# Thirty of 1661 gathers of edge rows, fetched row by row from SyncE's queue instead of by GpSimd

## The chip, the cores and the metric

The kernel runs on one core of a Trainium2 chip. The metric is the device time of one execution in microseconds (us); the runs of one kernel are summed up by their median.

## What is computed

A graph layer, a linear-attention mixer and a mixture of experts over 12500 nodes of 256 features. The change lies in the graph layer, with 212500 edges that are sorted by destination:

```python
h = einsum('ni,hif->hnf', x, W)                    # 8 heads of 32
s_src, s_dst = einsum('hnf,hf->hn', h, a_src), einsum('hnf,hf->hn', h, a_dst)
ea = leaky_relu(s_src[:, src] + s_dst[:, dst]).T   # one score per edge and head
ea = exp(ea - segment_max(ea, dst)[dst])
ea = ea / (segment_sum(ea, dst)[dst] + EPS)
out = segment_sum(hn[src] * ea[:, :, None], dst)   # sum over a node's edges
```

The mixer's result and the layer's input are added, and the sum goes through eight experts, two per node.

## The kernel before, in words

The program has three stages with a barrier between them. In the first, each node gets a row of 272 numbers in a table in memory (`table`: 256 features, 16 scores). In the second, the edge stage, the edges are taken in 104 groups of 16 chunks of 128 edges. In the third, nodes are routed to experts, and the experts run.

The edge stage is written out by hand, engine by engine:

- GpSimd (`edges_pool`, L1232) gathers the 128 table rows of each chunk with one indirect DMA, by row numbers that lie in `srcix`. There are three buffers `rows`, one per group (`NR` = 3); the gather of chunk j of group k waits until PE has summed chunk j of group k - 3.
- ScalarE (`copy_scores`, L1348) copies the scores out of a group's rows once all 16 gathers have landed; for group k + 2 it does so at the end of its iteration k. PE transposes them (L1296), VectorE makes edge scores and maxima and weighs the rows (L1463), PE sums each chunk with a one-hot matrix (L1314), ScalarE copies the sums out (L1370) and sends them to memory (L1395, L1398).
- SyncE (`edges_sync`) has one iteration per group. It loads the edge numbers of group k + 2 (`dsr`, L1260), takes three steps of other work, reads a flag (`anyfar`, L1273) that tells whether a node in this group has so many edges that its sums have to be moved, and takes a fourth step.

The other work is that of the mixer: on every engine, `Beside` takes steps of the mixer's weights (L821), its network with 25 blocks of nodes (on SyncE L1015 loads, L1020 stores, L1032 loads) and of the merge behind it. The steps are counted, so that a step stands at the same place of the groups on all engines. SyncE waits in its one stream: what stands behind a wait is issued after it.

```python
for k in range(GROUPS):
    if NR <= k + 2 < GROUPS:
        edge_ids(sp, S, B, k + 2)
    for _ in range(3):
        beside()
```

Of the kernel before, what the change touches and what calls it, by code (L numbers as in the profile page):

```python
# [63 lines left out]

LAG, TURN_LAG, TURN_GAP = 7, 12, 7

ROUNDS = [list(range(k, min(k + 2, NS))) for k in range(0, NS, 2)]
# [69 lines left out]
class Sems:  # L139
    def __init__(self, nc):  # L140
        new = nc.alloc_semaphore
        several = lambda name, n: [new(f"{name}{i}") for i in range(n)]
        self.stage = new("stage_done")
        self.const = new("constants")
        self.vec = new("vector_chain")

        self.ix_in, self.ix_rows, self.ix_fl = new("ix_in"), new("ix_ends_out_in"), new("ix_first_last")
        self.ix_tp, self.ix_cp, self.ix_num = new("ix_turned"), new("ix_copied"), new("ix_numbers")
        self.ix_hot, self.ix_hist, self.ix_sums = new("ix_hot_ready"), new("ix_histogram"), new("ix_sums")

        self.a_w, self.a_x, self.a_xt, self.a_h = new("a_weights_in"), several("a_x_in", NXB), several("a_xt_in", NXB), several("a_h_out", NXB)
        self.wcat, self.a_zero = new("wcat_ready"), new("frag_zeroed")
        self.xn, self.xnt, self.xt, self.h, self.hr, self.gram = (new(n) for n in (
            "norms_ready", "rows_turned", "xt_copied", "h_done", "h_copied", "gram_done"))
        self.gcopy = new("gram_copied")

        self.mix_in, self.mixp, self.mixv, self.mixa = new("mix_in"), new("mix_tensor"), new("mix_vector"), new("mix_scalar")

        self.es_in, self.es_sd, self.es_tp = new("ends_in"), new("ends_scores_copied"), new("ends_moved")

        self.rows_in, self.ds_in = several("rows_in", NR), several("ds_in", NR)
        self.near, self.far = several("near_out", 2), several("far_out", 2)
        (self.sce, self.tsc, self.flags, self.oh, self.inb, self.eav, self.fm, self.exp, self.tw, self.tail, self.wgh,
         self.sum, self.ev) = (new(n) for n in (
            "scores_copied", "scores_turned", "flags_ready", "onehot_ready", "scores_free", "edge_scores", "maxima_ready", "weights_exp",
            "weights_turned", "tails_ready", "rows_weighed", "chunk_summed", "chunk_copied"))

        self.m_w, self.m_xs, self.m_xt, self.m_o = new("m_weights_in"), new("m_x_in"), new("m_xt_in"), new("m_out")
        (self.m_pre, self.m_ready, self.m_q, self.m_x2, self.m_hn, self.m_tp, self.m_t, self.m_f1, self.m_g, self.m_f2, self.m_y,
         self.m_x3) = (new(n) for n in (  # L170
            "m_bias_sum", "m_weights_ready", "m_q_done", "m_x2_ready", "m_hn_ready", "m_hn_turned", "m_hnt_copied", "m_fc1_done",
            "m_gelu_done", "m_fc2_done", "m_y_added", "m_x3_ready"))

        self.mg_in, self.mg_out = new("mg_in"), new("mg_out")
# [12 lines left out]
        self.e_endrow, self.planned = new("e_end_rows"), new("planned")  # L187

        self.x_w1, self.x_w, self.x_b = new("x_first_weights_in"), new("x_second_weights_in"), new("x_biases_in")
        self.x_in, self.x_y, self.x_wt = several("x_in", NI), several("x_out", NOUT), new("x_first_weights_copied")  # L190
        self.x_wc, self.x_bc = several("x_wc_in", NW), several("x_bc_in", NB)
        (self.x_tp, self.x_gt, self.x_f1, self.x_h, self.x_f2, self.x_st, self.x_aim) = (new(n) for n in (
            "x_turned", "x_in_copied", "x_fc1_done", "x_gelu_done", "x_fc2_done", "x_y_read_scaled", "x_aimed"))
# [80 lines left out]
class Bufs:  # L274


    def __init__(self, nc, a, out):
# [17 lines left out]
        self.wqa, self.bqa = A("wqa", [P, KD, D], F32), A("bqa", [P, D], F32)  # L295
        self.dfb, self.dlb, self.loc = A("dfb", [GH, CHUNKS], F32), A("dlb", [GH, CHUNKS], F32), A("loc", [P, CHUNKS], F32)
        self.srcix, self.sdedge = A("srcix", [P, CHUNKS], I32), A("sdedge", [P, 2, GROUPS], F32)
        self.begins = A("ends_begins", [P, BLOCKS], F32)
        self.norm = A("norm", [P, 2, TILES], F32)
        self.far, self.anyfar, self.islast = A("far", [1, CHUNKS], I32), A("anyfar", [1, GROUPS], I32), A("islast", [P, CHUNKS], BF16)  # L300
        mark = nc.sbuf_base
        self.fli = A("dfl_i", [P, 2, BLOCKS], I32)
        mark_ix = nc.sbuf_base

        self.rows = several("rows", NR, [P, CB, ROW])
# [3 lines left out]
        self.onehot = several("onehot", 2, [P, CB, P])  # L309
        mark_ends = nc.sbuf_base  # L310
        self.ends, self.sd = A("ix_rows", [P, BLOCKS, ROW], F32), A("ix_sd", [P, 2, BLOCKS, GH], F32)
        ends_end, nc.sbuf_base = nc.sbuf_base, mark_ends
        self.fout = several("fout", 2, [P, CB, ROW])
        mark_edges = nc.sbuf_base
# [17 lines left out]
        self.wcat, self.avec = A("wcat", [P, KD, ROW], F32), A("avec", [P, 2, D], F32)  # L332
        self.xs, self.st_a = several("xs", NXB, [P, 2 * ST, D]), A("st_a", [P, 2 * ST, 16], F32)
        self.xt, self.hr = several("xt", NXB, [P, KD, ST * P]), several("hr", NXB, [P, ST, ROW])
        self.shift = A("ix_shift", [P, 2 * P], F32)

        nc.sbuf_base = mark_edges
        self.dsr, self.sc_e = several("dsr", NR, [P, 2, P], I32), several("sc_e", 2, [P, 2, P])
# [15 lines left out]
        self.m_xt, self.m_x2 = A("m_xt", [P, KD, ST * P], F32), several("m_x2", 2, [P, ST, D])  # L354
        self.m_hn, self.m_xs = (A(n, [P, ST, D], F32) for n in ("m_hn", "m_xs"))
        self.m_hnt, self.m_hid, self.m_st = A("m_hnt", [P, KD, ST * P], F32), A("m_hid", [P, MT, ST * P], F32), A("m_st", [P, ST, 16], F32)

        nc.sbuf_base = mark_mlp
        self.first, self.last = several("mg_first", 2, [P, 4, ROW]), several("mg_last", 2, [P, 4, ROW])
# [865 lines left out]
def edges_pool(p, S, B, groups):  # L1225
    for k in groups:
        b = k % NR
        for j in range(min(CB, REAL - k * CB)):
            col = k * CB + j
            if k >= NR:  # L1230
                p.wait_ge(S.sum, (k - NR) * CB + j + 1)
            p.indirect_dma_start(out=B.rows[b][:, j, :], out_offset=None, in_=B.table[:, :],  # L1232
                                 in_offset=bass.IndirectOffsetOnAxis(ap=B.srcix[:, col:col + 1], axis=0)).then_inc(S.rows_in[b], 16)
# [26 lines left out]
        sp.dma_start(B.dsr[b][:, j, :], bass.AP(of.tensor, k * CB * P, [[P, CB], [0, GH], [1, P]])).then_inc(S.ds_in[b], 16)  # L1260


def edges_sync(sp, S, B):
    beside = Beside(mix_sync(sp, S, B), mlp_sync(sp, S, B), merge_sync(sp, S, B))
    for k in range(GROUPS):
        if NR <= k + 2 < GROUPS:
            edge_ids(sp, S, B, k + 2)
        for _ in range(3):
            beside()

        b = k % 2
# [69 lines left out]
def edges_scalar(a, S, B):  # L1341
    beside = Beside(mix_scalar(a, S, B), mlp_scalar(a, S, B), merge_scalar(a, S, B))

    def copy_scores(k):
        r, b = k % NR, k % 2
        a.wait_ge(S.rows_in[r], 16 * (CB * (k // NR) + min(CB, REAL - k * CB)))
        a.wait_ge(S.tsc, max(k - 1, 0))
        a.activation(B.sc_e[b][:, :, :].rearrange("p j (c h) -> p j c h", h=GH),  # L1348
                     B.rows[r][:, :, D:ROW].rearrange("p c (j h) -> p j c h", h=GH), ACT.Copy).then_inc(S.sce, 1)
# [1116 lines left out]
    late(route_scalar(a, S, B), experts_scalar(a, S, B))  # L2466


def sync_program(sp, S, B):
    nodes_sync(sp, S, B)  # L2470
    barrier(sp, S, 1)
    for k in range(NR):
        edge_ids(sp, S, B, k)
    edges_sync(sp, S, B)
    barrier(sp, S, 2)
    late(route_sync(sp, S, B), experts_sync(sp, S, B))
    for q in range(NF):
        sp.wait_ge(S.e_x1[q], max(stored_to(r) for r in range(q, len(ROUNDS), NF)))
    for u in range(NOUT):
        sp.wait_ge(S.x_y[u], added_to(max(range(u, SLOTS, NOUT))))  # L2480


def build(nc, a, out):
# [2 lines left out]
    vector_program(nc.vector, S, B)  # L2486
    tensor_program(nc.tensor, S, B)
    scalar_program(nc.scalar, S, B)
    sync_program(nc.sync, S, B)


_INS = ["x", "src", "dst", "L0_gnn_W", "L0_gnn_a_src", "L0_gnn_a_dst", "L0_mix_w_qkv", "L0_mix_b_qkv",
# [26 lines left out]
```

## Time and profile before

| | us |
|---|---|
| median of 3 runs | 3769.97 |
| lowest and highest run | 3769.4, 3783.53 |
| span of the profiled execution, first to last instruction | 3246.6 |
| median less span | 523.4 |

The profiled execution's own time is not listed beside its span. In the span, PE is busy 81%, GpSimd 69%, VectorE 62% and ScalarE 48%; the edge stage runs from about 153 us to 2290 us.

Rows of the trace name line, engine (PE and PEld for TensorE's products and weight loads, DVE for VectorE, ACT for ScalarE, POOL for GpSimd, SP for SyncE; a q behind it is the engine's sequencer, which issues DMAs and does register work), operation, output<-input and count.

### The profile page before, as it was taken

How to read it: one execution, taken by the hardware profiler on the slowest of the kernel's cores; microseconds unless marked ns; L12 is line 12 of the kernel's file. 1: busy time of each engine (PE TensorE's matmuls, PEld its weight loads, DVE VectorE, ACT ScalarE, POOL GpSimd, SP SyncE). 2: the span in 40 equal slices, each digit the busy share in tenths (PEclk: the TensorE clock that was granted, in tenths of full speed). 3: DMA queues.
4: the chain of work that ended last, by engine and by line, in shares of the span. 5: the costliest groups of instructions: out<-in, count | busy, mean ns of one | idle time of the engine just before them, and what ended most of it. 6: DMA issues, size and time to landing. Idle time of an engine off the chain costs nothing.

```text
span 3246.6 us, 42100 instructions
## 1 busy us (share of the span) xinstructions
PE 2642.4 (81%) x11512; PEld 2052.3 (63%) x11512; DVE 2010.3 (62%) x5442; ACT 1549.7 (48%) x3382; POOL 2234.9 (69%) x2193
## 2 busy tenths in 40 slices
PE   8657767888888888888888887566359999999998
PEld 6546655666666665666656656344247888778887
DVE  7446557667777676777767766677654555445422
ACT  5325544544555554555455554334234545545444
POOL 0277777777777777777777777776476767676554
PEclk9879988999999999999999998777569999999999
DMA  9797766566666666666566665565766676766663
GB/s 276 242 295 211 199 178 169 162 173 177 164 172 180 172 172 170 174 179 171 163 180 172 173 169 153 160 181 136 253 198 146 151 160 148 162 142 131 131 110 62
DMA packets 397637, 561.15 MB, mean 173 GB/s; under 512 B 71912, under 2 KB 317950, under 8 KB 397225
## 3 DMA queue, kind: packets, MB, share of 16 engines
q0 software_dynamic: 123696, 298.61, 36.3%
q1 hardware_dynamic: 196473, 170.69, 18.1%
q10 hardware_dynamic: 77159, 88.50, 10.4%
q8 instruction: 99, 1.62, 0.2%
q14 instruction: 210, 1.72, 0.2%
HBM read 402.42 MB, written 169.68 MB: 176 GB/s over the span
## 4 chain that ended last, share of the span: by engine, by line
PE 65%; DMA 10%; ACT 8%; POOL 8%; issue 6%; DVE 2%; ACTq 0%; SPq 0%; POOLq 0%; DVEq 0%
PE bank L1314 21%; PE bank L2295 11%; PE bank L2308 10%; DMA rows<-table,srcix 9%; PE bank L1095 7%; POOL rows L1232 6%; PE bank L1084 5%; PE bank L1057 2%; PE bank L865 1%; PE bank L605 1%; PE bank L606 1%; ACT L1354 1%; PE bank L2284 1%; ACT xg L842 1%; PE bank L1296 1%
## 5 line engine op out<-in xcount | busy, mean ns | idle before, releaser
L1232 POOL DMA_INDIRECT rows<-table,srcix x1661 | 1600.3, 963 | 506.4 <-issue 354.2
L1314 PE MATMUL bank<-rows,onehot 128*128 128x272 f32 x3328 | 928.6, 426 | 57.4 <-ACT fout L1370 52.0
L1370 ACT ACTIVATE fout<-bank 128x272 f32<-128x272 f32 x1659 | 638.6, 397 | 574.7 <-PE bank L1314 525.3
L1314 PEld LDWEIGHTS bank<-rows,onehot 128*128 128x128 f32 x3328 | 666.5, 208 | 244.3 <-ACT fout L1370 78.7
L1463 DVE TENSOR_TENSOR rows<-rows,bank 128x1024 f32<-128x1024 f32 x416 | 484.0, 1213 | 173.2 <-ACT rows L1359 172.8
L2386 POOL DMA_INDIRECT out<-x_y,x_dest x203 | 325.0, 1601 | 233.2 <-DMA out<-x_y,x_dest 173.4
L2295 PE MATMUL bank<-x_int,x_w1c 128*128 128x256 f32 (+1 forms) x1696 | 379.7, 378 | 25.5 <-issue 22.2
L2308 PE MATMUL bank<-e_w,x_ht 128*128 x1624 | 370.5, 381 | 9.5 <-issue 7.0
L2295 PEld LDWEIGHTS bank<-x_int,x_w1c 128*128 128x128 f32 x1696 | 316.4, 194 | 77.4 <-issue 35.6
L2334 ACT ACTIVATE x_ht<-bank,x_b1c 128x256 f32<-128x256 f32 (+1 forms) x424 | 173.1, 462 | 394.4 <-PE bank L2295 392.9
L2308 PEld LDWEIGHTS bank<-e_w,x_ht 128*128 128x128 f32 x1624 | 300.2, 190 | 51.3 <-issue 14.8
L1084 PE MATMUL bank<-m_hnt,fc_w 128*128 128x512 f32 (+1 forms) x600 | 284.0, 598 | 17.1 <-ACT m_hid L1200 17.1
L2363 DVE TENSOR_TENSOR x_y<-bank,x_b2c 128x512 f32<-128x512 f32 (+1 forms) x106 | 70.8, 668 | 341.1 <-PE bank L2308 341.1
L1296 PE MATMUL bank<-ident,sc_e 128*128 128x128 f32 x104 | 38.4, 369 | 286.4 <-ACT sc_e L1348 275.4
L1095 PE MATMUL bank<-fc_w,m_hid 128*128 128x256 f32 x1176 | 270.8, 382 | 0.0
L1436 DVE SCALAR_TENSOR_TENSOR g_sdm<-notself,bank 128x128 f32<-128x128 f32 x104 | 30.0, 288 | 360.6 <-PE bank L1297 360.1
L1348 ACT ACTIVATE sc_e<-rows 128x256 f32<-128x256 f32 x104 | 43.3, 416 | 435.4 <-DMA rows<-table,srcix 417.3
L1095 PEld LDWEIGHTS bank<-fc_w,m_hid 128*128 128x128 f32 x1176 | 226.1, 192 | 34.2
L1771 POOL DMA_INDIRECT sorted_d<-e_hn,e_row x196 | 195.5, 997 | 64.9 <-issue 58.2
L1428 DVE TENSOR_TENSOR onehot<-bank,loc 128x2032 f32<-128x2032 f32 x104 | 235.6, 2266 | 0.2
L1296 PEld LDWEIGHTS bank<-ident,sc_e 128*128 128x128 f32 x104 | 16.4, 158 | 326.2 <-ACT sc_e L1348 313.7
L1084 PEld LDWEIGHTS bank<-m_hnt,fc_w 128*128 128x128 f32 x600 | 118.0, 198 | 112.3 <-issue 74.4
(405 smaller groups left out, 3246.3 us busy)
## 6 DMA issues: line engine op xcount, KB each, us to landing
frag<-fout ACTq DMA_DIRECT2D x104, 544.0 KB
rows<-table,srcix POOLq DMA_INDIRECT x1661
x_in<-sorted_d SPq DMA_DIRECT2D x97, 260.0 KB, 3.5
x_b2c<-in_L_ffn_b SPq DMA_DIRECT2D x106, 128.0 KB, 3.5
frag<-in_x ACTq DMA_DIRECT2D x1, 13416.0 KB
table<-hr SPq DMA_DIRECT2D x24, 544.0 KB, 4.0
xs<-in_x SPq DMA_DIRECT2D x24, 512.0 KB, 6.0
xg<-in_x SPq DMA_DIRECT2D x24, 512.0 KB, 6.4
```

Source lines behind the costliest of these rows:

```text
L1084: t = pe.matmul(bank[own[m % 2]][:, 0:n * P], B.mw1[:, kk, m * P:(m + 1) * P], B.m_hnt[:, kk, 0:n * P], start=(kk == 0), stop=(kk == KD - 1))
L1095: t = pe.matmul(bank[own[i // 2]][:, i % 2 * D:(i % 2 + 1) * D], B.m_hid[:, m, i * P:(i + 1) * P], B.mw2[:, m, :], start=(m == 0), stop=(m ...
L1232: p.indirect_dma_start(out=B.rows[b][:, j, :], out_offset=None, in_=B.table[:, :], in_offset=bass.IndirectOffsetOnAxis(ap=B.srcix[:, col:c ...
L1314: pe.matmul(B.banks[2 + c % 3][:, 0:ROW], B.onehot[k % 2][:, j, :], B.rows[k % NR][:, j, :], start=True, stop=True).then_inc(S.sum, 1)
L1370: a.activation(B.fout[k % 2][:, j, :], B.banks[2 + c % 3][:, 0:ROW], ACT.Copy).then_inc(S.ev, 1)
L1428: v.tensor_tensor(B.onehot[b][:, :, 0:P - 1], B.banks[0][:, 2 * P:3 * P - 1].unsqueeze(1).to_broadcast([P, CB, P - 1]), B.loc[:, k * CB:(k ...
L1463: v.tensor_tensor(h, h, w.unsqueeze(3).to_broadcast([P, n, GH, GF]), ALU.mult).then_inc(S.wgh, 1)
L1771: p.indirect_dma_start(out=B.sorted_d[:, :], out_offset=bass.IndirectOffsetOnAxis(ap=B.e_row[:, j, at:at + 1], axis=0), in_=B.e_hn[r % NH] ...
L2295: t = pe.matmul(out, B.w1c[u][:, k, m * P:(m + 1) * P], B.gt[u][:, k, 0:n], start=(k == 0), stop=(k == KD - 1))
L2308: t = pe.matmul(bk[BANKS_OUT[u]][:, i * D:(i + 1) * D], B.ht[u][:, m, i * P:(i + 1) * P], B.w2[:, bass.ds(ex * HT + m, 1), :], start=(m == ...
L2334: a.activation(B.ht[u][:, m, 0:n], B.banks[BANKS_H[m * 2 // HT]][:, m % 2 * ET:m % 2 * ET + n], ACT.Gelu, bias=B.b1c[w][:, m:m + 1]).then_ ...
L2386: p.indirect_dma_start(out=B.out[:, :], out_offset=bass.IndirectOffsetOnAxis(ap=B.dest[j % (NOUT + 1)][:, i:i + 1], axis=0), in_=B.y[j % N ...
```

## The change

SyncE fetches the first chunk of 30 groups: group 4 and every third after it, up to group 91. GpSimd leaves these chunks out.

Before the first group, three loads put the row numbers of the 30 chunks in partitions 1 to 3 of `far`. In three iterations of SyncE, nine steps are taken for one chunk, one ahead of each of the three beside steps: eight that load 16 row numbers into 16 registers and issue 16 DMAs of one row each into a buffer `hand` (two of these), and a ninth that waits for the 128 rows and for the group's buffer, and copies them to their place. The chunk of group k = 4 + 3i is fetched in the iterations 3i to 3i + 2, that is k - 4 to k - 2. The values carry no range check. ScalarE's copy of the scores of such a group also waits for the move. Three small tensors are put elsewhere in the on-chip memory to make room.

```diff
+HAND_FIRST, HAND_EVERY, HANDS = 4, 3, 30
+HAND_PART = 16
...
 def edges_pool(p, S, B, groups):
     for k in groups:
         b = k % NR
-        for j in range(min(CB, REAL - k * CB)):
+        for j in range(0 if hand_of(k) is None else 1, min(CB, REAL - k * CB)):
...
+def hand_sync(nc, sp, S, B):
+
+    step = HAND_EVERY * CB * P
+    for row in range(HAND_ROWS):
+        first, n = row * HAND_IDS, min(HAND_IDS, HANDS - row * HAND_IDS)
+        sp.dma_start(B.far[1 + row:2 + row, 0:n * P].rearrange("o (c e) -> o c e", e=P),
+                     bass.AP(B.src.tensor, HAND_FIRST * CB * P + first * step, [[step * n, 1], [step, n], [1, P]])).then_inc(S.ix_in, 16)
+    sp.wait_ge(S.ix_in, 32 + 16 * HAND_ROWS)
+    for i in range(HANDS):
+        b, row, at, k = i % 2, 1 + i // HAND_IDS, i % HAND_IDS * P, HAND_FIRST + i * HAND_EVERY
+        if i >= 2:
+            sp.wait_ge(S.sce, k - 2 * HAND_EVERY + 1)
+        for part in range(HAND_PARTS):
+            e0 = part * HAND_PART
+            _, ids = nc.values_load_multi_w_load_instructions(
+                B.far[row:row + 1, at + e0:at + e0 + HAND_PART], engines=[mybir.EngineType.SP], min_val=0, max_val=N_PAD - 1,
+                skip_runtime_bounds_check_because="ids of the padded table's rows")
+            for e, of in enumerate(ids, e0):
+                sp.dma_start(B.hand[b][e:e + 1, :], B.table[bass.ds(of, 1), :]).then_inc(S.hand_rows[b], 16)
+            yield
+        sp.wait_ge(S.hand_rows[b], 16 * P * (i // 2 + 1))
+        sp.wait_ge(S.sum, (k - NR) * CB + 1)
+        sp.dma_start(B.rows[k % NR][:, 0, :], B.hand[b][:, :]).then_inc(S.hand, 16)
+        yield
...
         for _ in range(3):
+            next(hand, None)
             beside()
...
-        a.wait_ge(S.rows_in[r], 16 * (CB * (k // NR) + min(CB, REAL - k * CB)))
+        a.wait_ge(S.rows_in[r], gathered_to(k))
+        if hand_of(k) is not None:
+            a.wait_ge(S.hand, hand_moved(hand_of(k)))
```

SyncE's stream where the edge stage begins, before: the edge numbers of three groups, then the mixer's first loads.

```order
L1260 DMA dsr<-in_dst 128x1x128
L1260 DMA dsr<-in_src 128x1x128
L821 DMA xg<-in_x 128x4x256 x2
L826 DMA wqkv_s<-in_L_mix_w_qkv 128x2x768
L827 DMA bqkv_row<-in_L_mix_b_qkv 1x768
```

The same place of SyncE's stream in the change (`far` holds the row numbers; ISA is the register operation that makes an address, FUSED_REGOPS in the profile):

```order
L1282 DMA dsr<-in_dst 128x1x128
L1282 DMA dsr<-in_src 128x1x128
L1290 DMA far<-in_src 1x13x128 x2
L1290 DMA far<-in_src 1x4x128
L1299 TENSOR_LOAD far
L1303 ISA
L1303 DMA hand<-table 1x272
L1303 ISA
L1303 DMA hand<-table 1x272
```

The pair of ISA and DMA stands there 16 times, then come the mixer's loads, then the next load of 16 numbers. In all the stream has 3840 such pairs, 240 loads and 30 moves more.

The end of a chunk in SyncE's stream of the change, in the third iteration:

```order
L1303 ISA
L1303 DMA hand<-table 1x272
L1307 DMA rows<-hand 128x272
L843 DMA xg<-in_x 128x4x256
L1323 TENSOR_LOAD anyfar
L1323 ISA x2
L1324 COMPARE_AND_BRANCH
```

The move is the last step of the chunk, ahead of the beside step and the flag of that iteration.

ScalarE's stream at the end of its iteration 2, before (with the semaphores that a row waits for):

```order
L1370 ACTIVATE fout0<-bank4 128x272 [waits chunk_summed]
L1395 DMA frag<-fout0 32x16x272 [waits chunk_copied]
L1398 DMA last_d<-fout0 1x4352
L1348 ACTIVATE sc_e0<-rows1 128x256 [waits scores_turned,rows_in1]
L1370 ACTIVATE fout1<-bank2 128x272 [waits chunk_summed,far_out1,near_out1]
```

And in the change:

```order
L1422 ACTIVATE fout0<-bank4 128x272 [waits chunk_summed]
L1447 DMA frag<-fout0 32x16x272 [waits chunk_copied]
L1450 DMA last_d<-fout0 1x4352
L1400 ACTIVATE sc_e0<-rows1 128x256 [waits scores_turned,a_xt_in_and_hand_moved0,rows_in1]
L1422 ACTIVATE fout1<-bank2 128x272 [waits chunk_summed,far_out1,near_out1]
```

The copy of the scores of group 4 waits for the move as well; behind it in ScalarE's stream stand the copies of the sums of group 3. On GpSimd, the row of 1661 gathers has become one of 1631.

## Rows read from the trace of the kernel before

**Rows 1.** Busy time by stretch: length, then each engine's busy us (instructions), PE's granted clock, DMA share, GB/s.
```profile
core 0: us, PE busy (x) PEld busy (x) DVE busy (x) ACT busy (x) POOL busy (x), PEclk, DMA share, GB/s
153.00:2243.00 2090.00, 1660.96 (x6611) 1225.70 (x6612) 1422.00 (x3113) 1021.05 (x2341) 1587.36 (x1649) 0.90 0.64 178
...
1080.00:2010.00 930.00, 794.62 (x3131) 582.28 (x3130) 658.66 (x1490) 486.13 (x1066) 706.01 (x735) 0.94 0.62 171
2010.00:2290.00 280.00, 173.38 (x654) 126.58 (x652) 197.85 (x382) 107.24 (x282) 191.03 (x193) 0.78 0.57 153
```

**Rows 2.** The gathers, by tile (ns min/median/max, first and last start) and in the page's groups.
```profile
L1232 POOL DMA_INDIRECT rows<-table,srcix x1661: 942/949/1988, 153.3 to 2258.6; - x185
...
L1232 POOL DMA_INDIRECT rows<-table,srcix x1661 | 1600.3, 963 | 506.4 <-issue 354.2
```

**Rows 3.** Who waited for whom: us in total, times, longest us.
```profile
ACT sc_e L1348 <- DMA rows<-table,srcix: 417.3, 82, 50.0
...
PE bank L1296 <- ACT sc_e L1348: 275.4, 65, 17.4
...
POOL rows L1232 <- PE bank L1314: 152.1, 499, 0.3
```

**Rows 4.** The same view for SP's own queue.
```profile
SPq L1015 <- PE bank L1057: 648.4, 24, 32.5
SPq L1020 <- DVE m_x L1153: 554.2, 25, 45.2
...
SPq L821 <- PE bank L865: 208.7, 22, 46.9
```

**Rows 5.** Lines L1830 and L1831 on SP: ns min/median/max, first and last start us.
```profile
L1830 SPq TENSOR_LOAD <-pl_endrow x8: 267/270/1007, 3073.5 to 3082.1; - x8
L1830 SPq FUSED_REGOPS  x8: 152/152/156, 3073.8 to 3082.4; - x8
...
L1831 SPq FUSED_REGOPS  x8: 37/37/42, 3074.0 to 3082.7; - x8
L1831 SPq DMA_DIRECT2D sorted_d<-pl_zero x8: 332/332/383, 3074.2 to 3082.9; - x8
...
DMA to landing us min/median/max: 2.1/3.2/4.5
```

**Rows 6.** SP's DMA issues in order of time (start, us), 1008 to 1042; line L1273.
```profile
1010.26 0.60 SPq L1260 DMA_DIRECT2D dsr<-in_src  x1
1036.02 0.38 SPq L1020 DMA_DIRECT2D xm_d<-m_x  x1
1036.44 0.50 SPq L1032 DMA_DIRECT2D m_xs<-in_x  x1
1038.41 0.59 SPq L1260 DMA_DIRECT2D dsr<-in_dst  x1
...
1040.55 0.55 SPq L1260 DMA_DIRECT2D dsr<-in_dst  x1
1041.14 0.60 SPq L1260 DMA_DIRECT2D dsr<-in_src  x1
...
L1273 SPq TENSOR_LOAD <-anyfar x104: 262/278/1197, 218.2 to 2255.8; - x104
```

**Rows 7.** Issues of other lines: ns min/median/max, first and last start us.
```profile
L732 SPq DMA_DIRECT2D dfb<-rows_d x1: 270/270/270, 48.1 to 48.1; - x1
L732 SPq DMA_DIRECT2D dlb<-rows_d x1: 298/298/298, 48.4 to 48.4; - x1
...
L1398 ACTq DMA_DIRECT2D last_d<-fout x103: 357/363/543, 224.1 to 2272.9; - x103
...
L1020 SPq DMA_DIRECT2D xm_d<-m_x x25: 370/378/383, 628.6 to 2027.9; - x25
L1032 SPq DMA_DIRECT2D m_xs<-in_x x25: 500/505/2418, 546.6 to 1972.7; - x25
...
L1521 SPq DMA_DIRECT2D mg_last<-fout x1: 603/603/603, 2284.0 to 2284.0; - x1
```

More of the change, by code:

```diff
@@ L65, with hand_of @@
 LAG, TURN_LAG, TURN_GAP = 7, 12, 7
+HAND_FIRST, HAND_EVERY, HANDS = 4, 3, 30
+HAND_PART = 16
+HAND_PARTS = P // HAND_PART
+HAND_IDS = CHUNKS // P
+HAND_ROWS = -(-HANDS // HAND_IDS)
+def hand_of(k):
+    i, off = divmod(k - HAND_FIRST, HAND_EVERY)
+    return i if off == 0 and 0 <= i < HANDS else None
 ROUNDS = [list(range(k, min(k + 2, NS))) for k in range(0, NS, 2)]
@@ L121, in added_to, with gathered_to, hand_moved @@
     return sum(16 * SUBS[i] for i in range(j % NOUT, j + 1, NOUT))
+def gathered_to(k):
+    return sum(16 * (min(CB, REAL - g * CB) - (hand_of(g) is not None)) for g in range(k % NR, k + 1, NR))
+def hand_moved(i):
+    return 16 * len(LOADED[0::NXB]) + 16 * (i + 1)
 def rows_of(a, s, n):
@@ L149, in __init__ @@
         self.ix_hot, self.ix_hist, self.ix_sums = new("ix_hot_ready"), new("ix_histogram"), new("ix_sums")
-        self.a_w, self.a_x, self.a_xt, self.a_h = new("a_weights_in"), several("a_x_in", NXB), several("a_xt_in", NXB), several("a_h_out", NXB)
+        self.a_w, self.a_x, self.a_xt, self.a_h = new("a_weights_in"), several("a_x_in", NXB), several("a_xt_in_and_hand_moved", NXB), several("a_h_out", NXB)
         self.wcat, self.a_zero = new("wcat_ready"), new("frag_zeroed")
@@ L161, in __init__ @@
         self.rows_in, self.ds_in = several("rows_in", NR), several("ds_in", NR)
+        self.hand_rows, self.hand = several("hand_rows_in", 2), self.a_xt[0]
         self.near, self.far = several("near_out", 2), several("far_out", 2)
@@ L297, in __init__ @@
         self.srcix, self.sdedge = A("srcix", [P, CHUNKS], I32), A("sdedge", [P, 2, GROUPS], F32)
-        self.begins = A("ends_begins", [P, BLOCKS], F32)
         self.norm = A("norm", [P, 2, TILES], F32)
-        self.far, self.anyfar, self.islast = A("far", [1, CHUNKS], I32), A("anyfar", [1, GROUPS], I32), A("islast", [P, CHUNKS], BF16)
-        mark = nc.sbuf_base
-        self.fli = A("dfl_i", [P, 2, BLOCKS], I32)
+        self.far, self.anyfar, self.islast = A("far", [1 + HAND_ROWS, CHUNKS], I32), A("anyfar", [1, GROUPS], I32), A("islast", [P, CHUNKS], BF16)
         mark_ix = nc.sbuf_base
@@ L311, in __init__ @@
         self.ends, self.sd = A("ix_rows", [P, BLOCKS, ROW], F32), A("ix_sd", [P, 2, BLOCKS, GH], F32)
+        self.begins, self.fli = A("ends_begins", [P, BLOCKS], F32), A("dfl_i", [P, 2, BLOCKS], I32)
+        self.shift = A("ix_shift", [P, 2 * P], F32)
         ends_end, nc.sbuf_base = nc.sbuf_base, mark_ends
@@ L334, in __init__ @@
         self.xt, self.hr = several("xt", NXB, [P, KD, ST * P]), several("hr", NXB, [P, ST, ROW])
-        self.shift = A("ix_shift", [P, 2 * P], F32)
         nc.sbuf_base = mark_edges
@@ L356, in __init__ @@
         self.m_hnt, self.m_hid, self.m_st = A("m_hnt", [P, KD, ST * P], F32), A("m_hid", [P, MT, ST * P], F32), A("m_st", [P, ST, 16], F32)
+        self.hand = several("hand", 2, [P, ROW])
         nc.sbuf_base = mark_mlp
@@ L1260, in edge_ids, with edges_sync @@
         sp.dma_start(B.dsr[b][:, j, :], bass.AP(of.tensor, k * CB * P, [[P, CB], [0, GH], [1, P]])).then_inc(S.ds_in[b], 16)
-def edges_sync(sp, S, B):
+def hand_sync(nc, sp, S, B):
[21 more added lines that the diff above has]
+        yield
+def edges_sync(nc, sp, S, B):
     beside = Beside(mix_sync(sp, S, B), mlp_sync(sp, S, B), merge_sync(sp, S, B))
+    hand = hand_sync(nc, sp, S, B)
     for k in range(GROUPS):
@@ L2466, in scalar_program, with sync_program @@
     late(route_scalar(a, S, B), experts_scalar(a, S, B))
-def sync_program(sp, S, B):
+def sync_program(nc, sp, S, B):
     nodes_sync(sp, S, B)
@@ L2473, in sync_program @@
         edge_ids(sp, S, B, k)
-    edges_sync(sp, S, B)
+    edges_sync(nc, sp, S, B)
     barrier(sp, S, 2)
@@ L2488, in build @@
     scalar_program(nc.scalar, S, B)
-    sync_program(nc.sync, S, B)
+    sync_program(nc, nc.sync, S, B)
 _INS = ["x", "src", "dst", "L0_gnn_W", "L0_gnn_a_src", "L0_gnn_a_dst", "L0_mix_w_qkv", "L0_mix_b_qkv",
```

## The prediction

> **What bounds the kernel now.** I read first the window table [rows 1]. The 2090 us from 153 to 2243 hold the edge stage, all but its last group; the node stage before and the expert stage behind keep their instructions, so the change is decided in this window. There POOL has 1587 us of busy time, PE 1661, DVE 1422, ACT 1021. None is full by that count, so the second view is the gathers themselves [rows 2]: 1661 of them start between 153.3 and 2258.6, one every (2258.6 - 153.3)/1660 = 1.268 us. The page's group gives the two parts of that pitch: 963 ns of work and 506.4 us of idle time over all gathers, 354.2 us of it "issue", the gap in which POOL waits for nothing. Third come the waits [rows 3]: ACT's copy of a group's scores waits 417 us for gathers that land, and PE's transposes of those scores wait for ACT; the other way, POOL waits 152 us for PE, in 499 pieces of at most 0.3 us. So POOL is the pacemaker: a group of 16 gathers lasts 20.29 us, three groups 60.9 us. A gather less is worth at most its pitch.
>
> SP has next to no work here, and yet is not free: it waits 648 us at L1015 (24 times), 554 us at L1020 and 209 us at L821 [rows 4], because the second network's loads and stores stand in its one stream at fixed steps beside the edges.
>
> **What the change removes.** 30 gathers of POOL: 30 x 1.268 = 38.0 us, if POOL stays the pacemaker and nothing arrives later. That is the whole possible gain, 1.0% of the time.
>
> **What it adds, all on SP's stream.** For one group in three, SP does the following in three of its iterations. In the meantime POOL uses 60.9 us, or 59.6 with the gather gone. What SP needs is the question.
>
> *128 row fetches.* Each is one FUSED_REGOPS (37 to 42 ns, [rows 5]), one DMA issue, and the gaps between instructions. A gap: the issue of dsr at 1040.55 lasts 0.55 and the next starts at 1041.14, so 0.04 us [rows 6]. The trace has no issue of one row with its address in a register. The nearest from above is L1831, 128 rows at a register's address, 332 ns [rows 5]; eight rows cost 270 and 298 (L732), the first one the lowest issue here [rows 7]. From below: L1398 is a piece of a single run, 363 ns, but stands right behind another issue. Such a place costs 0.505 - 0.378 = 0.127 us on SP (L1032 behind L1020), which leaves 0.236 us. I take 0.25, between 0.236 and 0.27, since a row has fewer parts than any of these. A row is then 0.04 + 0.25 + 2 x 0.04 = 0.37 us, 128 rows 47.4 us; the bounds are 45.6 us with 0.236 and 57.9 us with 0.332.
>
> *8 register loads of 16 numbers.* The trace has only loads of one number: 278 ns for L1273, 270 for L1830 [rows 5, 6]. If 16 come in one trip, the load costs 0.28 us; if they are 16 whole loads, 4.45 us. I expect one trip per number, because a one-number load takes seven times as long as the 37 ns register operation beside it, and only the trip to memory tells them apart. Of the 0.278 us I put down 0.152 (the other multi-step register instruction, [rows 5]) as what is paid once and 0.126 per number: 0.15 + 16 x 0.126 = 2.17 us. With its gap 2.21, times 8: 17.7 us. The bounds are 2.6 and 35.9 us.
>
> That is the least known term. The Trainium skill (Runtime: NRT & Kernel Launch, "Instruction fetch mechanics") says that a load into sequencer registers costs about 200 ns per register "even for bulk"; no run here shows a load of several. By it a load would be 3.2 us, the eight 25.9, and the kernel would end near 4416 us instead of the time below.
>
> *The wait and the move.* SP waits until the last row has landed: L1831's writes land 2.1 to 4.5 us after issue, 3.2 in the middle [rows 5]; the beside work in between hides a little, so 2.5 us. The move of 128 rows is one static issue, 0.5 us with its gap, priced like L1260. Its wait for the sum of an earlier group costs nothing as long as SP is the late one.
>
> *What SP does already.* Two dsr issues, the anyfar load and the branch: 2.14 us from 1038.41 to 1040.55, an iteration without anything else [rows 6], 6.4 us for three. The second network's three issues (0.378 + 0.378 + 0.505 and gaps) come 25 times in some 75 groups: 1.4 us for three groups.
>
> The sum: 47.4 + 17.7 + 2.5 + 0.5 + 6.4 + 1.4 = **75.9 us of SP against 60.9 us of POOL.** The move is waited for by ACT (the group's scores), ACT by PE, DVE and in the end POOL, whose buffers come free with PE's sums. So SP becomes the pacemaker, 15.0 us later with every hand, and the gathers saved on POOL are worth nothing: POOL then waits for buffers. Over 30 hands that is +450 us. Two credits: at the start SP sat up to 46.9 us at L821 [rows 4], so about 25 us of the first hand cost nothing; at the end POOL stands up to three buffers ahead, and the last twelve groups win back about 25 us before POOL paces again. Net +400 us: span 3246.6 + 400 = 3647 us.
>
> What else moves: the copy of 128 rows inside the chip and 30 gathers less are small beside the 0.64 DMA share [rows 1] and are covered by it; if rows on one queue were served late, the landing term grows. The three loads of row numbers lie ahead of the stage's first group and go with the start credit. The moved buffers cost nothing, no instruction hangs on their place. PE's share falls as SP paces; the window from 2010 to 2290, with PE busy 173 of 280 us, has a mean granted clock of 0.78, against 0.94 in the window before it with 795 of 930 [rows 1]. PE's 1661 us at 0.90 would be 1916 at 0.78, still under the 2490 us that the stage would then last, so I cost that at nothing; its cover is SP's own pace.
>
> The median of the runs shown is 3769.97 us, 523.4 us above the profiled span; the profiled execution's own time is not listed, so the median stands for it and these 523.4 us are held fixed. Forecast: 3769.97 + 400 = **4170 us**.
>
> **The rivals.**
> 1. *SP keeps up (faster).* If the 16 numbers come in one trip (2.6 us for eight) and a row costs 0.36 us or less, SP needs 45.6 + 2.6 + 10.8 = 59.0 us, under POOL's 59.6. It decides at 48.8 us for rows and loads together. Then the 38 us are had: 3732 us. For it: nothing in the trace forbids a cheap one-row issue or a block load. Against it: SP would be 99% full, and its stream still stops at L1015 and L1020 until PE and DVE have come to the same step (from about 1010.9 to 1036.0 in [rows 6]); every such stop would make a hand late. Chance 0.13.
> 2. *One trip per load, but SP just full.* Rows at 0.37, loads at 2.6: 60.8 us, to which the stops at L1015 and L1020 add some 2 us a hand on average, where one falls into the first iteration after a move, before PE has moved on. 62.8 - 60.9, times 30, less the 50 us of credits, is +7 us; with 5 us of stops +97. I put it at 3825 us, between the two; a row at 0.40 adds 3.8 us a hand and makes it 3940. Chance 0.24, of which 0.09 lies within 0.5% of the time before.
> 3. *Dearer than forecast.* 16 whole trips (35.9 us) give 94.1 us a hand, 30 x 33.2 - 50 = +946 us: 4716 us. Issues as dear as L1831's give 10.5 us more a hand: +315 us on any case. [...] Chance 0.13.
>
> That the change doesn't do what it says can be left out: the order of the instructions shows 1631 gathers, 3840 fetches and 30 moves.
>
> **How the numbers follow.** The forecast (SP paces, a trip per number, 1 to 3.3 us a load, its own range 3890 to 4600 us, the top with dearer rows) has chance 0.50. About 0.5%, some 19 us, is what a measurement can tell from no change here. Faster by more: rival 1, 0.13. Within: 0.09, from rival 2. Slower: 0.78. The range from 3725 to 4600 us takes in rivals 1 and 2 and the forecast's own range, and leaves out most of rival 3 and the tails.
>
> **What would show it.** Right: SP's fetches back to back, pitch near 0.37 us, with a load of about 2.2 us ahead of each 16; the waits at L1015 and L1020 nearly gone; ACT's score copies waiting long for the move's landing once in three groups, while POOL waits for PE's sums; a group pitch near 25 us up to group 91, then 20. Wrong: a load of 0.3 us or a row pitch under 0.36 (rivals 1, 2), POOL's pitch unchanged at 1.27 us with no new wait (rival 1), or the time outside the span growing with the longer program.

## The result, and the profile after the change

| | us |
|---|---|
| before, median of 4 runs (3763.11 to 3783.53) | 3769.68 |
| after, median of 4 runs (4749.42 to 4781.26) | 4764.19 |
| after / before | 1.2605, interval 1.2558 to 1.2652 |
| span of the profiled execution after, and its time | 4754.2, 4755.46 |

The change makes the kernel slower by 994.5 us, where +400 was forecast; the time lies above the range. The profiled execution ends 1.3 us after its span, so nothing like 523.4 us lies outside the span of a run; the profile of before that was shown, with its span of 3246.6 us, is that of an execution some 490 us or more shorter than every timed run.

SP's instructions for the hands in the changed kernel, by line (ns min/median/max, first and last start in us; L1299 loads 16 registers, L1303 fetches rows, L1307 moves them):

```profile
L1299 SPq TENSOR_LOAD <-far x240: 5/1159/3500, 165.1 to 3374.7; - x120
...
L1303 SPq FUSED_REGOPS  x3840: 1/37/1422, 166.3 to 3382.4; - x192
L1303 SPq MOVE hand<-table x3840: 1/29/1407, 166.4 to 3382.4; - x192
L1303 SPq DMA_DIRECT2D hand<-table x3840: 1/225/1696, 167.1 to 3382.5; - x192
...
L1307 SPq DMA_DIRECT2D rows<-hand x30: 533/542/1006, 320.0 to 3383.8; - x30
```

The 30 moves start from 320.0 to 3383.8: a hand takes (3383.8 - 320.0)/29 = 105.6 us, where the prediction had 75.9. The medians are small, the maxima are not, and even a register operation of 37 ns has one of 1.4 us. A row is three instructions: the address operation, a MOVE and the issue. Over all 3840 rows, from the start of an instruction to the start of the next in the trace, the address operation takes 648.4 us, the MOVE 628.2 and the issue 1287.1: 2563.7/3840 = 0.668 us a row in the mean, though the medians of the three are 0.073 + 0.060 + 0.276 = 0.41 us. The trace in order of time (start, us) shows both paces within 20 us:

```profile
999.67 2.44 SPq L1303 DMA_DIRECT2D hand<-table  x7
1004.39 0.60 SPq L1282 DMA_DIRECT2D dsr<-in_dst  x1
1005.04 0.59 SPq L1282 DMA_DIRECT2D dsr<-in_src  x1
1006.87 9.58 SPq L1303 DMA_DIRECT2D hand<-table  x12
```

Six steps between seven rows in 2.44 us are 0.41 us each; eleven in 9.58 us are 0.87. In the second stretch many of SP's instructions, register operations too, start about 0.70 us after the one ahead.

Who waited for whom in the changed kernel (us in total, times, longest us), answering to [rows 3]:

```profile
POOL rows L1254 <- PE bank L1364: 1394.5, 371, 48.3
ACT sc_e L1400 <- DMA rows<-hand: 787.3, 29, 38.0
...
PE bank L1346 <- ACT sc_e L1400: 684.0, 41, 39.5
DVE g_sdm L1488 <- PE bank L1347: 568.4, 55, 23.3
DVE m_x L1141 <- DMA xm_d<-m_x: 407.8, 16, 38.5
...
DVE neq L1471 <- DMA dsr<-in_src: 319.9, 32, 22.5
```

The order of the engines has turned round. ACT waits for 29 of 30 moves, PE for ACT's scores, and POOL, which waited 152.1 us for PE in pieces of at most 0.3 us [rows 3], now waits 1394.5 us in pieces of up to 48.3. SP is late with its other work too: DVE waits for the second network's stores and for the edge numbers. SP itself no longer stops; its one wait among the edges that the view still lists is

```profile
SPq L1307 <- DMA hand<-table: 25.9, 27, 1.1
```

The 648.4 us at L1015, 554.2 at L1020 and 208.7 at L821 [rows 4] are gone. On the page, 44% of the chain that ended last lies with SP, and the gathers' idle time has grown from 506.4 us [rows 2] to 1926.7:

```profile
SPq 44%; issue 27%; PE 20%; another core or an unknown queue 2%; DVE 2%; ACT 2%; DMA 2%; ACTq 0%; POOL 0%; DVEq 0%; POOLq 0%
SPq L1303 32%; PE bank L2360 7%; PE bank L2347 7%; SPq L1299 6%; SPq L1282 2%; PE bank L1364 2%; SPq L1323 2%; PE bank L627 1%; PE bank L628 1%; PE bank L2336 1%; DMA hand<-table 1%; ACT x_ht L2386 1%; ACT e_hn L1951 0%; DMA out<-x_y,x_dest 0%
...
L1254 POOL DMA_INDIRECT rows<-table,srcix x1631 | 1559.6, 956 | 1926.7 <-PE bank L1364 1394.5
```

The gathers last to 3639.0 us, and up to the last move, at about 3384, no engine is full (by stretch: length, busy us of each engine, granted clock, DMA share, GB/s), as in [rows 1] but thinner:

```profile
L1254 POOL DMA_INDIRECT rows<-table,srcix x1631: 940/946/1706, 154.0 to 3639.0; - x182
...
143.00:3384.00 3241.00, 1723.14 (x6115) 1215.78 (x6115) 1271.50 (x2805) 920.67 (x2118) 1399.12 (x1467) 0.77 0.39 107
```

### The profile page after: what moved, and what is told of

Same layout as the page of the kernel before. It is cut to its first block, busy times and chain, and to the rows that moved or that the text cites. A ratio compares the mean times of both kernels' runs of the same rounds, so it can differ in the third digit from the quotient of the medians.

```text
span 4754.2 us, 53893 instructions
## 1 busy us (share of the span) xinstructions
PE 2882.8 (61%) x11512; PEld 2160.2 (45%) x11512; DVE 2019.6 (42%) x5442; ACT 1534.5 (32%) x3382; POOL 2191.3 (46%) x2163
## 4 chain that ended last, share of the span: by engine, by line
SPq 44%; issue 27%; PE 20%; another core or an unknown queue 2%; DVE 2%; ACT 2%; DMA 2%; ACTq 0%; POOL 0%; DVEq 0%; POOLq 0%
SPq L1303 32%; PE bank L2360 7%; PE bank L2347 7%; SPq L1299 6%; SPq L1282 2%; PE bank L1364 2%; SPq L1323 2%; PE bank L627 1%; PE bank L628 1%; PE bank L2336 1%; DMA hand<-table 1%; ACT x_ht L2386 1%; ACT e_hn L1951 0%; DMA out<-x_y,x_dest 0%
## 5 line engine op out<-in xcount | busy, mean ns | idle before, releaser
L1254 POOL DMA_INDIRECT rows<-table,srcix x1631 | 1559.6, 956 | 1926.7 <-PE bank L1364 1394.5
L1364 PE MATMUL bank<-rows,onehot 128*128 128x272 f32 x3328 | 1040.8, 457 | 419.0 <-ACT fout L1422 312.5
L1364 PEld LDWEIGHTS bank<-rows,onehot 128*128 128x128 f32 x3328 | 695.8, 221 | 678.9 <-ACT fout L1422 369.5
L1422 ACT ACTIVATE fout<-bank 128x272 f32<-128x272 f32 x1659 | 621.0, 397 | 1176.7 <-PE bank L1364 698.3
L1346 PE MATMUL bank<-ident,sc_e 128*128 128x128 f32 x104 | 38.1, 366 | 721.7 <-ACT sc_e L1400 684.0
L2360 PE MATMUL bank<-e_w,x_ht 128*128 x1624 | 386.5, 392 | 9.1 <-issue 7.1
L1106 PE MATMUL bank<-m_hnt,fc_w 128*128 128x512 f32 (+1 forms) x600 | 314.1, 652 | 44.4 <-ACT m_hid L1222 38.3
L2360 PEld LDWEIGHTS bank<-e_w,x_ht 128*128 128x128 f32 x1624 | 311.4, 197 | 56.6 <-issue 15.5
L1117 PE MATMUL bank<-fc_w,m_hid 128*128 128x256 f32 x1176 | 288.5, 400 | 0.0
L1117 PEld LDWEIGHTS bank<-fc_w,m_hid 128*128 128x128 f32 x1176 | 240.0, 204 | 40.6
L1079 PE MATMUL bank<-wqa,m_xt 128*128 128x256 f32 x392 | 125.9, 478 | 196.5 <-DMA m_xt<-in_xT 151.9
```

Of the source, the lines that this page charges most:

```text
L1106: t = pe.matmul(bank[own[m % 2]][:, 0:n * P], B.mw1[:, kk, m * P:(m + 1) * P], B.m_hnt[:, kk, 0:n * P], start=(kk == 0), stop=(kk == KD - 1))
L1117: t = pe.matmul(bank[own[i // 2]][:, i % 2 * D:(i % 2 + 1) * D], B.m_hid[:, m, i * P:(i + 1) * P], B.mw2[:, m, :], start=(m == 0), stop=(m ...
L1364: pe.matmul(B.banks[2 + c % 3][:, 0:ROW], B.onehot[k % 2][:, j, :], B.rows[k % NR][:, j, :], start=True, stop=True).then_inc(S.sum, 1)
L1422: a.activation(B.fout[k % 2][:, j, :], B.banks[2 + c % 3][:, 0:ROW], ACT.Copy).then_inc(S.ev, 1)
L2360: t = pe.matmul(bk[BANKS_OUT[u]][:, i * D:(i + 1) * D], B.ht[u][:, m, i * P:(i + 1) * P], B.w2[:, bass.ds(ex * HT + m, 1), :], start=(m == ...
```

## The experiments

All runs but the first edit the changed kernel. Where a ratio is given, it is to runs of the kernel before on the same chip; a run without one was timed once.

**The kernel before, once more.** No edit.

> The kernel before, profiled beside the others. In the changed kernel the span (4754.2 us) ends 1.3 us short of the time (4755.46 us), while the profile of the kernel before has a span of 3246.6 us against runs near 3770 us. If 523 us of every run of the kernel before lie outside its span, this run shows a span near 3247 us again. If its runs and that profiled execution are two different things, the span comes out near 3769 us, and the question is which stretch is longer: the node stage, the edge stage (2090 us in the profile shown) or the expert stage (956 us).

Measured: 3780.78 us, ratio 1.0003 (0.9977 to 1.0028), profiled span 3783.3 us. The gathers there, by tile and in the page's groups, beside [rows 2]:

```profile
L1232 POOL DMA_INDIRECT rows<-table,srcix x1661: 943/949/1941, 154.6 to 2659.3; - x185
...
L1232 POOL DMA_INDIRECT rows<-table,srcix x1661 | 1599.9, 963 | 906.1 <-issue 366.4
...
POOL rows L1232 <- PE bank L1314: 321.1, 368, 19.4
```

The work of a gather is the same 963 ns; the idle time between them is 906.1 us, not 506.4. The pitch is (2659.3 - 154.6)/1660 = 1.509 us, so a group takes 24.14 us and three take 72.4, not 60.9. POOL waits for PE here too, 321.1 us in pieces of up to 19.4, so the 1394.5 us of the changed kernel are to be held against this rather than against [rows 3]. The 523.4 us thus lie inside the stages: 399.4 among the edges (2504.7 from the first gather to the last, against 2105.3), the rest behind them. SP's line L1273 in this execution:

```profile
L1273 SPq TENSOR_LOAD <-anyfar x104: 3/280/1145, 244.2 to 2671.4; - x104
L1273 SPq FUSED_REGOPS  x104: 3/154/717, 244.7 to 2671.7; - x104
```

The median of the load is that of [rows 6], 280 ns against 278, but its minimum was 262 there and is 3 here: SP's instructions come in fits in the kernel before too. Of its register and semaphore instructions, loads aside, 112 last over 400 ns, against 2 in the trace shown first.

SP is not alone in this. ScalarE's copies of the sums, in the trace shown first, in this run, and in the run with small copies in place of the gathers that follows below ("remote" is a release that the view puts down to no instruction, "issue" idle time without a wait):

```profile
L1370 ACT ACTIVATE fout<-bank 128x272 f32<-128x272 f32 x1659 | 638.6, 397 | 574.7 <-PE bank L1314 525.3 <-DMA last_d<-fout 4.8 <-SPq L1283 3.9
...
L1370 ACT ACTIVATE fout<-bank 128x272 f32<-128x272 f32 x1659 | 619.4, 397 | 1155.5 <-PE bank L1314 542.2 <-remote 450.5 <-issue 139.8
...
L1425 ACT ACTIVATE fout<-bank 128x272 f32<-128x272 f32 x1659 | 639.4, 397 | 647.1 <-PE bank L1367 604.1
```

The 450.5 and 139.8 us of idle time that no instruction accounts for stand in neither the trace shown first nor the one with small copies. So in the kernel as timed ScalarE, too, loses time beside the gathers.

What follows: a hand has to be held against 72.4 us, and (105.6 - 72.4) x 30 = +996 us, beside +994.5 measured. That the two agree to 2 us is chance: the profiled spans differ by 4754.2 - 3783.3 = 970.9 us.

**Rows fetched, but not used.** POOL gathers all 1661 chunks; SP fetches the rows of the 30 hands and drops them; there is no move, and ACT waits for none.

```diff
...
-        for j in range(0 if hand_of(k) is None else 1, min(CB, REAL - k * CB)):
+        for j in range(min(CB, REAL - k * CB)):
...
-        sp.wait_ge(S.sum, (k - NR) * CB + 1)
-        sp.dma_start(B.rows[k % NR][:, 0, :], B.hand[b][:, :]).then_inc(S.hand, 16)
...
-        if hand_of(k) is not None:
-            a.wait_ge(S.hand, hand_moved(hand_of(k)))
```

> SP fetches the 30 x 128 rows as in the changed kernel and waits for them, but no one uses them: GpSimd gathers all 1661 chunks, there is no move and ScalarE waits for none. Theory (SP's stream paces by its length, about 105 us a hand in the changed kernel): SP is just as late, and its edge numbers (dsr) and the second network's loads hold the others: 4550 to 4760 us. Rival (the wait for the move is the whole cost): the edge stage runs at GpSimd's pace again and the time is that of the kernel before, within 1.5%.

Measured: 4697.87 us. With nobody waiting for a row, the kernel is nearly as slow. Who waited for whom in this run:

```profile
POOL rows L1254 <- PE bank L1362: 1342.1, 419, 61.2
...
DVE m_x L1141 <- DMA xm_d<-m_x: 665.7, 23, 42.7
DVE neq L1467 <- DMA dsr<-in_src: 496.4, 42, 20.6
...
PE bank L1079 <- DMA m_xt<-in_xT: 260.7, 23, 22.9
```

The lateness comes through SP's old work, which stands behind the fetches in its one stream. The wait for the move is one way of several in which it reaches the others; without it this one run is 66 us shorter.

**One copy in place of the fetches.** POOL leaves the 30 gathers out; SP makes one plain copy of 128 fixed rows per hand, straight to its place. Left out: fetching the right rows.

```diff
...
-            for e, of in enumerate(ids, e0):
-                sp.dma_start(B.hand[b][e:e + 1, :], B.table[bass.ds(of, 1), :]).then_inc(S.hand_rows[b], 16)
...
-        sp.dma_start(B.rows[k % NR][:, 0, :], B.hand[b][:, :]).then_inc(S.hand, 16)
+        sp.dma_start(B.rows[k % NR][:, 0, :], B.table[i * P:(i + 1) * P, :]).then_inc(S.hand, 16)
```

> GpSimd leaves the 30 chunks out; instead of rows by number SP copies 128 fixed rows of the table to the chunk's place in one issue at the step of the move, so the edges of these chunks get other rows. This is the gain without its price. Theory (GpSimd paces the edge stage with 1.268 us a gather): 38 us less than before, 3732 us. Rival (PE, ScalarE and VectorE are so close behind that a gather less frees nothing): within 10 us of the kernel before.

Measured: 3754.78 us, ratio 0.9935 (0.9906 to 0.9964), 22 us under the 3776.76 us of the kernel before beside it. With SP nearly free, 30 gathers less are worth 22 us (14 to 35 by the interval), not 38: between the two expectations. POOL also waits for PE here, which would explain that not every gather left out shortens a group; no run tests that.

```profile
POOL rows L1254 <- PE bank L1357: 373.4, 378, 19.8
```

**128 fixed rows, without registers.** Rows at fixed addresses: no loads, no register operations, but as many issues. Left out: fetching the right rows.

```diff
...
-            for e, of in enumerate(ids, e0):
-                sp.dma_start(B.hand[b][e:e + 1, :], B.table[bass.ds(of, 1), :]).then_inc(S.hand_rows[b], 16)
+            for e in range(e0, e0 + HAND_PART):
+                sp.dma_start(B.hand[b][e:e + 1, :], B.table[i * P + e:i * P + e + 1, :]).then_inc(S.hand_rows[b], 16)
```

> As the changed kernel, but the 128 rows of a hand are fixed rows of the table: no load of row numbers and no register operation, 128 issues a hand instead of 128 issues, 256 register instructions and 8 loads. The edges of these chunks get other rows. In the changed kernel a row takes 0.41 us in the middle, but 0.84 us on average, because every so often the instructions of SP, register operations and issues alike, take 0.7 us each for some 10 us. Theory A (the stretches of 0.7 us go with the number of instructions that SP gets through): 128 x 0.27 + 14 + 13 = 61 us a hand, SP is just about full, 3770 to 3900 us. Theory B (they go with the number of transfers on SP's queue): 34 + 41 + 13 = 88 us a hand, about 4250 us.

Measured: 3801.41 us, within the range of Theory A. The moves come every (2399.3 - 287.3)/29 = 72.8 us, the pace of the kernel before, and SP again waits for others:

```profile
L1300 SPq DMA_DIRECT2D hand<-table x3840: 2/248/10700, 162.1 to 2398.2; - x192
...
SPq L1037 <- PE bank L1079: 79.3, 13, 10.2
SPq L1037 <- remote: 73.9, 10, 14.2
```

An issue alone still costs 0.457 us from start to start in the mean, 0.294 in the median: these are disturbed as well, though the mean also holds some of SP's waits. With 128 instructions a hand instead of 384 and the loads, the fetches take 128 x 0.457 = 58.5 us of SP, and it keeps up. (The changed kernel's mean row is 0.668 us; the 0.84 of the expectation was too high.)

**Small copies instead of gathers.** From the fourth group on (k = 3; the expectations of two later runs call it the fifth) POOL copies one fixed row per chunk instead of gathering 128. Left out: the gathering.

```diff
+            if k >= NR:
+                p.dma_start(B.rows[b][0:1, j, :], B.table[0:1, :]).then_inc(S.rows_in[b], 16)
+                continue
```

> As the changed kernel, but from the fourth group on GpSimd copies one fixed row for each chunk instead of gathering 128 (the groups weigh old rows again; the fetched chunks are as before). SP's stream, its waits and everybody's waits for buffers stay. In the changed kernel SP's instructions take 0.7 us each just while gathers are moving (the gathers' queue has 5.4 us of packets per us then, 1.5 otherwise). Theory (the gathers' transfers slow SP's instructions, whatever these are): a row comes back to 0.41 us on average, a hand from 105.6 to 75 us, the time to 3800 to 3950 us. Rival (SP is slowed by its own program or its own transfers): the mean row stays near 0.67 us and the time above 4500 us.

Measured: 3947.85 us, the upper end of what the theory allowed. SP's program is unchanged, and its rows and moves are now:

```profile
L1306 SPq FUSED_REGOPS  x3840: 37/37/1397, 164.9 to 2635.4; - x192
L1306 SPq MOVE hand<-table x3840: 3/29/709, 165.0 to 2635.5; - x192
...
L1310 SPq DMA_DIRECT2D rows<-hand x30: 533/542/1618, 294.2 to 2637.0; - x30
```

A row takes (314.1 + 262.2 + 1210.5)/3840 = 0.465 us in the mean, and a hand (2637.0 - 294.2)/29 = 80.8 us. Of the 3840 address operations 3 take between 0.65 and 0.8 us to the start of the next instruction, against 341 in the changed kernel. So it is GpSimd's gathers that slow SP, though a row does not come back all the way to 0.41; without them SP is still the pacemaker (ACT waits 668.2 us for moves), near the 75.9 us that were predicted.

**Half the hands.** 15 chunks, one in six groups, a step of the hand at every second place: half the work for SP per group.

```diff
-HAND_FIRST, HAND_EVERY, HANDS = 4, 3, 30
+HAND_FIRST, HAND_EVERY, HANDS = 7, 6, 15
...
-        for _ in range(3):
-            next(hand, None)
+        for step in range(3):
+            if (3 * k + step) % 2 == 0:
+                next(hand, None)
```

> 15 chunks instead of 30, one group in six, each spread over six iterations of SP instead of three. Theory (what counts is SP's time for a hand against the time the others take for the groups between): 92 us of rows and loads and six iterations of the rest, some 120 us, against 145 us that six groups take here, so SP keeps up and the 15 gathers left out may show: between 3755 and 3790 us, no difference that can be measured. Rival (fetching by hand costs in proportion, wherever it stands): half of the 990 us, about 4270 us.

Measured: 3821.76 us, ratio 1.010 (1.007 to 1.013). A miss for either expectation, and the most telling one on the price of a row: it is not a constant. POOL now gathers at nearly the pace of the kernel before (24.8 us a group), and a row on SP costs (470.5 + 503.8 + 743.0)/1920 = 0.89 us in the mean. So half the fetches take two thirds of SP's time for all of them, and SP has little left over (28.9 + 27.4 us in these waits, against 648.4 and 554.2 in [rows 4]):

```profile
SPq L1037 <- PE bank L1079: 28.9, 4, 13.8
SPq L1042 <- DVE m_x L1175: 27.4, 3, 15.5
```

What stays nearly constant is SP's loss for each gather that GpSimd starts meanwhile. Above the medians, 0.409 us a row, the rows of the changed kernel lose 2563.7 - 3840 x 0.409 = 993 us, and half as many rows here 1717.3 - 1920 x 0.409 = 932 us. Between the first and the last fetch the trace has 1447 gathers there and 1458 here: 0.69 and 0.64 us a gather (the latter with some 36 us of SP's waits in it; without them 0.61). With small copies the same rows lose 1786.8 - 3840 x 0.409 = 216 us, 0.15 us a copy.

**Plain copies of as many bytes.** The same place in POOL's program, a copy of 128 neighbouring rows instead of one row. Left out: the gathering.

```diff
+            if k >= NR:
+                p.dma_start(B.rows[b][:, j, :], B.table[col % TILES * P:(col % TILES + 1) * P, :]).then_inc(S.rows_in[b], 16)
+                continue
```

> As the run with small gathers, but on GpSimd's queue each of its gathers from the fifth group on is replaced by a plain copy of 128 consecutive rows of the table into the same part of the buffer: as many bytes as a gather, with no list of row numbers and no scattered reads. The output weighs wrong rows: what is left out is the gathering. Theory A (it is the bytes that move through the DMA engines which make SP's instructions slow): a row still costs 0.6 to 0.9 us on SP, a hand about 105 us, the time is over 4400 us. Theory B (only the indirect gathers, with their scattered reads and lists, slow SP): a row costs 0.47 us as with the small gathers, a hand about 81 us, the time is about 3950 us.

Measured: 3945.14 us, as with the small copies; a row takes (312.1 + 262.3 + 1200.2)/3840 = 0.462 us, a hand 80.9. The page of this run, GpSimd's copies and its queue's packets:

```profile
q0 software_dynamic: 122256, 294.43, 27.7%
...
L1255 POOL DMA_DIRECT2D rows<-table x1583 | 841.7, 538 | 1772.0 <-PE bank L1367 1705.3
```

Packets and bytes are the same as in the changed kernel, whose page has

```profile
q0 software_dynamic: 122256, 294.43, 24.3%
```

Theory A falls: as many bytes and packets on GpSimd's queue do not slow SP as its gathers do.

**Narrow gathers, and gathers of sorted rows.** Two runs on what of a gather does it. The first keeps the lists and moves 32 bytes a number; the second makes the lists from the sorted destinations, so that a gather reads about eight neighbouring rows. Left out: the right rows.

```diff
+            if k >= NR:
+                p.indirect_dma_start(out=B.rows[b][:, j, 0:8], out_offset=None, in_=B.table[:, :].rearrange("n (k c) -> (n k) c", c=8),
+                                     in_offset=bass.IndirectOffsetOnAxis(ap=B.srcix[:, col:col + 1], axis=0)).then_inc(S.rows_in[b], 16)
+                continue
```

> From the fifth group on each of GpSimd's gathers is still an indirect DMA with its list of 128 row numbers, but each number fetches 32 bytes (eight numbers of the table seen as pieces of eight) instead of a row of 1088 bytes. The output weighs rows that are not the gathered ones: what is left out is the gathering of whole rows. The run with plain copies showed that as many bytes and packets without a list leave a row on SP at 0.47 us. Theory A (what slows SP is the list, the 128 scattered descriptors of an indirect DMA, whatever they move): a row still costs 0.6 to 0.9 us, a hand about 105 us, the time is over 4400 us. Theory B (it takes the scattered reading of whole rows): a row costs 0.47 us, a hand about 81 us, the time is about 3950 us.

```diff
-            for to, of in ((B.di, B.dst), (B.si, B.src)):
+            for to, of in ((B.di, B.dst), (B.si, B.dst)):
```

> The changed kernel with one word changed: GpSimd's lists are made from the destinations of the edges instead of their sources. The destinations are sorted, so a gather's 128 numbers name about eight neighbouring rows of the table over and over; the lists, the descriptors and the bytes are as many as before. The output is the sum of other rows: what is left out is fetching the sources' rows, outside of the 30 chunks that SP fetches. Theory A (it is the list, whatever it names): as the changed kernel, a row 0.67 us, a hand about 105 us, about 4750 us. Theory B (it is the reading all over the table): a row 0.47 us, a hand about 81 us, about 3950 us.

Measured: 4726.28 and 4705.72 us, rows of (642.1 + 616.8 + 1292.7)/3840 = 0.664 and (631.1 + 631.9 + 1275.0)/3840 = 0.661 us, hands of 105.0 and 104.4 us. GpSimd's queue moved a good quarter of the bytes in the narrow run,

```profile
q0 software_dynamic: 96928, 80.46, 10.2%
```

and a row on SP costs what it did in the changed kernel. Theory A holds in both: neither the bytes nor where the rows lie matters, but that GpSimd issues indirect DMAs, each with a list of 128 numbers. These do not slow SP in every execution: the trace of before that was shown first has the same 1661 gathers and next to none of the long instructions. Whether SP is disturbed by GpSimd's 0.95 us of work on a list (0.54 for a plain copy) or by what that work sends on was not tried and stays open.

## Why the prediction was wrong in size and right in direction

- **SP becomes the pacemaker: right.** The fetches run back to back, SP's waits of [rows 4] are gone, ACT waits for 29 moves, POOL for PE's sums. The run with unused rows adds what the prediction did not weigh: SP's lateness also reaches the other engines through its old loads and stores, and nearly as much without any move.
- **The price of one undisturbed row: nearly right.** The issue is 0.225 us where 0.25 was taken and 0.236 was the lower bound. That bound took off 0.127 us for a place right behind another issue, read from two different transfers (L1032 and L1020); in the run with fixed rows, issues right behind one another have a median of 0.248 us. What was left out is the MOVE ahead of each issue, 0.060 us with its gap. So a row is 0.41 us, not 0.37, which is 5 us a hand. The trace of before had it, at L1831 between the two lines of [rows 5]:

```profile
L1831 SPq MOVE sorted_d<-pl_zero x8: 29/29/29, 3074.1 to 3082.8; - x8
```

- **"A row is then 0.04 + 0.25 + 2 x 0.04 = 0.37 us, 128 rows 47.4 us": the step that failed most.** It took the durations of an idle SP for those of a busy one. Beside the gathers a row costs 0.668 us in the mean, and 0.89 where they come at nearly the pace of the kernel before; 128 rows are 85.5 us, above the upper bound of 57.9. Of these 33.1 us (993/30) lie above the medians. With small copies in place of the gathers 128 rows are 59.5 us, so 26.0 us a hand are what GpSimd's gathers hold SP up: a term that the sum did not have. The trace of before shows SP only in bursts of a few instructions and next to none of the long ones, so nothing in it was a burst of 384 slowed by gathers, and the upper bound was no bound.
- **16 registers to a load: the size was off, the other way.** Counted from start to start, a load takes 1.22 us, eight take 9.8 instead of 17.7. The instruction itself has a median of 1.159 us, and (1.159 - 0.278)/15 = 0.06 us for each further register, half the 0.126 assumed: between the price of one load and that of sixteen. By the figure of the Trainium skill (Runtime: NRT & Kernel Launch, "Instruction fetch mechanics"), some 200 ns a register, it would be 3.2 us. That page speaks of loads from HBM; this load, from on-chip memory, measured 1.159.
- **Landing, move, SP's own work: right.** 105.6 - 85.5 - 9.8 = 10.3 us, against 2.5 + 0.5 + 6.4 + 1.4 = 10.8. Of that the wait for the landing was 1 us.
- **"These 523.4 us are held fixed": failed.** They lie inside the stages. Three groups of the kernel as timed take 72.4 us, not 60.9. Taken alone, this would have made the change cheaper: with a hand of 75.9 us SP would have lost 3.5 us each, or about 105 us. That the loss came out larger all the same shows how far off the price of a row was.
- **The gain, 38 us: too large.** With SP nearly free, 30 gathers less are worth 22 us; that POOL's waits for PE are the reason is argued, not shown.
- **The credits of 50 us: mostly not seen.** From the first gather to the last, the changed kernel takes 3639.0 - 154.0 = 3485.0 us and the kernel before, run again, 2504.7: 980.3 us more, where 30 hands of 33.2 make 996. That leaves 16 us.
- **The clock: as costed.** From 143 to 3384 us the granted clock was 0.77 where 0.78 was put down, and PE's 1723 us of 3241 stayed covered.
- **The rivals.** The first two needed a row of 0.36 or 0.37 us and fell with it. The third, dearer than forecast, gave 4716 us and came nearest, though for another reason: dear rows, not dear loads. That its 33.2 us a hand (94.1 - 60.9) is also the measured 105.6 - 72.4 is luck.

The sum by term, forecast to measured: 75.9 + 38.1 (rows) - 7.9 (loads) - 0.5 (the rest) = 105.6 us a hand.

## What to carry to other kernels

Price a burst of instructions on an engine by a burst of the same kind in the trace, beside the work that will run beside it; the median of a few isolated ones leaves out what that other work costs. Then ask what the extra time goes with: here it went with the gathers that passed, not with the rows that were fetched, so half the rows cost two thirds of the time. Before a gap between the profiled span and the timed median is held fixed, find where it lies, since a pacemaker that is slower in the timed runs also has more slack. And an engine whose long waits look like room may have none: they say how long it stood still, not how fast its instructions come when it must not stand still.

## What the runs showed of the hardware

- In all but one of the traces with GpSimd's indirect gathers, SP's instructions come in stretches in which many start about 0.70 us after the one ahead, whatever they are; a row of three instructions costs 0.41 us between such stretches, 0.668 in the mean in the changed kernel and 0.89 with half the hands. What SP's rows lost above their medians was 0.69 and 0.64 us for each gather started meanwhile, against 0.15 for each small copy. Plain copies from the same queue with the same packets and bytes leave a row at 0.46. By which way the one holds up the other no run shows.
- ScalarE loses time beside the gathers too: 450.5 and 139.8 us of idle time before its copies of the sums that the trace puts down to no instruction, none of it listed where GpSimd made small or plain copies.
- Loading 16 registers from on-chip memory took 1.159 us against 0.278 for one; issuing a DMA of one row at a register's address 0.225 us against 0.332 for 128 rows [rows 5].
- The kernel before had an execution with a span of 3246.6 us, in which SP and ScalarE show next to none of this, beside timed runs of 3734.55 to 3805.72. Why that one was free of them stays open.
